# The middle fourteen steps of a fused pose, memory and expert kernel: loop or written out

## What is computed

```
# part 1, per frame: three graph attention layers over the 50 joints, 4 heads
for W, a_s, a_d, bg, R, g, b in layers:            # widths 3 -> 64 -> 128 -> 64
    h = x @ W                                       # per head
    e = leaky_relu(score_src[src] + score_dst[dst], 0.2)
    alpha = softmax of e over the edges that end in a joint
    out = sum over those edges of alpha * h[src]  + bg
    x = gelu(layer_norm(out + x @ R, g, b))
pose = layer_norm(x.reshape(frames, 50*64) @ fpW + fpb)
# part 2, per token (pose tokens and text tokens together, layer-normed)
q = l2norm(silu(causal_conv4(silu(x @ w_q1.T) @ w_q2.T)))
x = x + (silu(q @ mem_w1.T) @ mem_w2.T) @ w_out.T
# part 3, per token: 8 experts 128 -> 512 -> 128 with gelu, the two best of a router weighted
```

## Time and profile before

| | |
|---|---|
| median of 3 runs | 4858.85 us (4856.44 to 4862.07) |
| profiled execution | 4847.68 us |
| its span, first to last instruction | 4845.9 us |
| instructions recorded | 72897 |
| TensorE busy | 88% |
| VectorE busy | 73% |
| ScalarE busy | 54% |
| GpSimd busy | 13% |
| mean granted TensorE clock | 0.964 |

### The profile page before, as it was taken

The page is one execution under the profiler, slowest core; times in us unless marked ns, Lnnn a source line. Parts: engine busy times, 40 slices in busy tenths (PEclk is TensorE's granted clock), DMA queues, the critical chain, the costliest instruction groups (busy, mean ns, idle before and its releaser), DMA issues.

```text
span 4845.9 us, 72897 instructions
## 1 busy us (share of the span) xinstructions
PE 4262.9 (88%) x22774; PEld 1939.4 (40%) x22774; DVE 3549.6 (73%) x8027; ACT 2615.6 (54%) x3930; POOL 627.6 (13%) x746
## 2 busy tenths in 40 slices
PE   4687989898998988989988898988899898899988
PEld 4223343443434334343433434344343433434345
DVE  1577777877778877777887777787777887777762
ACT  0454655556565555655555565555555555565643
POOL 1111201111020111102011120111102011110100
PEclk9898999999999999999999999999999999999998
DMA  2000000000000000000000000000000000000000
GB/s 95 2 1 3 1 3 4 2 5 1 3 4 4 4 2 5 1 3 4 3 4 1 6 1 3 4 3 4 1 4 3 4 4 2 5 1 4 3 2 6
DMA packets 23087, 25.64 MB, mean 5 GB/s; under 512 B 3395, under 2 KB 21835, under 8 KB 22139
## 3 DMA queue, kind: packets, MB, share of 16 engines
q1 hardware_dynamic: 22650, 20.26, 1.3%
HBM read 16.06 MB, written 4.19 MB: 4 GB/s over the span
## 4 chain that ended last, share of the span: by engine, by line
PE 64%; DVE 18%; issue 8%; ACT 7%; POOL 1%; DVEq 0%; SPq 0%; DMA 0%; ACTq 0%; POOLq 0%
PE bank L859 11%; PE bank L812 8%; PE bank L925 7%; PE bank L916 6%; PE bank L696 5%; PE bank L829 4%; PE bank L770 3%; PE bank L850 2%; PE bank L815 2%; ACT X L1264 2%; PE bank L708 2%; DVE X L1870 2%; DVE Ho L2019 2%; PE bank L832 1%; PE bank L846 1%
## 5 line engine op out<-in xcount | busy, mean ns | idle before, releaser
L1870 DVE TENSOR_TENSOR X<-X,bank 128x1024 f32<-128x1024 f32 (+2 forms) x432 | 483.7, 1140 | 268.2 <-PE bank L736 153.2
L1264 ACT ACTIVATE X<-X,c_vec 128x1024 f32<-128x1024 f32 (+2 forms) x432 | 498.3, 1176 | 298.3 <-DVE X L1870 297.2
L1308 ACT ACTIVATE X<-bank,bgc 128x512 f32<-128x512 f32 (+1 forms) x624 | 419.2, 672 | 441.9 <-PE bank L859 441.9
L916 PE MATMUL bank<-XT,c_w 128*128 128x512 f32 x1024 | 509.6, 626 | 28.6 <-ACT SQ L1344 26.6
L925 PEld LDWEIGHTS bank<-c_w,SQ 128*128 128x128 f32 x4096 | 481.9, 192 | 56.5 <-issue 50.2
L925 PE MATMUL bank<-c_w,SQ 128*128 128x128 f32 x4096 | 500.8, 277 | 0.0
L812 PE MATMUL bank<-R,c_W 64*128 64x512 f32 (+1 forms) x832 | 473.3, 650 | 28.4 <-issue 23.3
L532 POOL TENSOR_TENSOR R<-X 128x512 f32<-128x512 f32 (+1 forms) x208 | 257.3, 1241 | 1613.4 <-PE bank L812 838.5
L859 PE MATMUL bank<-R,c_C 128*128 128x512 f32 (+1 forms) x832 | 460.2, 635 | 0.0
L846 PE MATMUL bank<-X,WR 64*128 64x512 f32 (+1 forms) x832 | 455.9, 637 | 0.0
L1344 ACT ACTIVATE SQ<-bank,c_vec 128x512 f32<-128x512 f32 x512 | 345.4, 686 | 164.6 <-PE bank L916 162.5
(11 more groups left out here) (258 smaller groups left out, 6822.5 us busy)
## 6 DMA issues: line engine op xcount, KB each, us to landing
c_w<-in_w SPq DMA_DIRECT2D x2, 2048.0 KB
out<-Ho SPq DMA_DIRECT2D x32, 128.0 KB, 2.6
c_fpW<-in_fpW SPq DMA_DIRECT2D x1, 3200.0 KB
X<-in_x SPq DMA_DIRECT2D x34, 75.0 KB, 1.9
X<-in_txt SPq DMA_DIRECT2D x32, 64.0 KB, 1.8
X<-in_chain SPq DMA_DIRECT2D x1, 1300.0 KB
X<-in_sel SPq DMA_DIRECT2D x1, 600.0 KB
X<-in_sel SPq DMA_DIRECT2D x1, 300.0 KB
```

Of the source, the lines that this page charges most:

```text
L916: mm(hidden_bank(e, m), w1[:, k * P:k * P + P], XT2[:], start=True, stop=True).then_inc(hid_ps, 1)
L1264: A_(dst, dst, ACT.Gelu, bias=v(f"b{l}"), scale=v(f"g{l}")).then_inc(x_ok, 1)
L1308: A_(dst, bZ[k % 2][:, 0:cols], ACT.Identity, bias=bias).then_inc(zs_ok, 1)
L1870: TT(dst, dst, b, ALU.mult).then_inc(u_ok, 1)
```

## The change

Each engine's loop over the steps 1 to 14 becomes a Python loop, so that the fourteen steps are written out one behind the other, with constants in place of the step register. The order of the work, the tiles and the waits stay as they are. On VectorE the counter that `link` waits for becomes a constant as well. The general path keeps its loops.

```
@@ SyncE
-                with sp.Fori(1, STEPS - 1) as s:
+                for s in range(1, STEPS - 1):
                     iteration(s, True, True)
@@ GpSimd
-                with pool.Fori(1, STEPS - 1) as s:
+                for s in range(1, STEPS - 1):
                     iteration(s, True)
@@ TensorE
-                with pe.Fori(1, STEPS - 1) as s:
+                for s in range(1, STEPS - 1):
                     iteration(s, True, True, True)
@@ ScalarE
-                with act.Fori(1, STEPS - 1) as s:
+                for s in range(1, STEPS - 1):
                     iteration(s, True, True)
@@ VectorE
-                with dve.Fori(1, STEPS - 1) as s:
+                for s in range(1, STEPS - 1):
                     start[0] = s * LINKS + (first - LINKS)
                     iteration(s, True, True)
```

## The result

The changed kernel took 4790.13 us (median of 4 runs, 4785.98 to 4797.39), the kernel before 4860.12 us beside it (4 runs): a ratio of 0.9863 [0.9845, 0.988]. Its profiled execution took 4790.66 us, 57.0 us less than that of before.

What follows compares the result with a forecast made beforehand. Engine work plus a pattern of low clock was taken to bound the kernel; 24.7 us for the jumps and 6.8 for the clock made 31.5, giving 4827 us from the median 4858.85, with a range of 4799 to 4853.

Steps and rivals of the forecast that it cites:

- What bounds the kernel: Whole kernel: engines' work fills the span; thirteen looped steps of 287.64 us each are work plus a pattern of low clock.
- The jump, 24.7 us: Loop's back edge on TensorE and VectorE: 13 jumps at 1.9 us each, all on the path, saved by writing out.
- Does the gain hold?: Claim that the lead at the layer's start, 2.09 us, survives to the first variance row (L1844), 2.05 us.
- Registers, nothing: Register instructions computing wait numbers in looped steps: costed at nothing, bound 0.2 us a step, 3 us over fourteen.
- The clock after the pause, 6.8 us: 13.7 us at clock 0.50 behind the restart in 5 of 13 boundaries: 1.4 us each, expected to go with the pause.
- the seam's further lead: Jump-free passage from fourteenth looped step to tail reaches L723 3.14 us earlier, 1.9 explained; the rest counted as nothing.
- The rival of the whole lead: All steps start like the jump-free seam: 47.6 us gain, 4811 us; at the shortest step length 59.4 us, 4799; chance 20%.
- The baseline: Gain summed against the profiled 4847.68 us but subtracted from the timed median 4858.85, 11.2 us above it, giving 4827.
- The slower rival: Clock pattern settles badly, every step falling into the long one: 12.5 us slower, 4871 us; chance 8%.
- The signs: Expected trace: no 3.6 us TensorE branch but the last, L1833 near 7.0 us, mean step near 285.2, busy times unchanged.

Runs made afterwards that it cites:

- e3: Kernel before with only VectorE's fourteen steps written out, the other engines keeping their loops: 4842.1 us, ratio 0.9984.
- e9: Kernel before with TensorE and VectorE written out with constants, loops of ScalarE, GpSimd and SyncE kept: 4806.9 us, ratio 0.9893.
- e5: Changed kernel with the step number taken from a register plus a constant on all engines but SyncE, no loop: 4819.6 us, ratio 0.9918.
- e12: Changed kernel with ten one-column memsets added at the end of each of VectorE's fourteen steps: 4801.2 us, ratio 0.9882.
- e14: Changed kernel with six small matmuls in layer 0's late waits, plus three at each of two waits in layers 1 and 2: 4793.4 us, ratio 0.9854.
- e13: Changed kernel with six small matmuls where TensorE waits late in layer 0's spreading: 4791.4 us, ratio 0.9851.
- e1: Changed kernel with each written-out step in a loop of one trip, its register replaced by constants: 4829.6 us, ratio 0.9935.
- e2: Kernel before with only TensorE's fourteen steps written out, the other four engines keeping their loops: 4911.2 us, ratio 1.0098.
- e6: Kernel before with the loop made seven trips of two steps on every engine, registers kept, six jumps back instead of thirteen: 4866.3 us, ratio 1.0014.
- e7: Kernel before with eight matmuls into a free bank at the end of TensorE's looped step: 4864.6 us, ratio 1.0002.
- e10: Changed kernel with two one-column memsets added at the end of each of VectorE's fourteen steps: 4795.2 us, ratio 0.9875.

## Why the prediction missed

*What bounds the kernel* was right: work plus a pattern of low clock, step by step. Two readings in it were loose. "The same to 1%" holds for VectorE and ScalarE, while TensorE's busy time went from 256.2 to 263.1 us with the clock; and the shortest step was 284.90 us, not 284.97.

*The jump, 24.7 us.* Right: 1.8 to 2.1 us a step at equal clock, 27 us at the most. VectorE's stall is what counts (e3); TensorE's 1.69 us are covered once that is gone, and the other engines' jumps are free on the path (e9).

The Trainium skill (Runtime: NRT & Kernel Launch, section Instruction fetch mechanics) says that a jump to code outside the two buffered blocks must fetch it first. The runs are on the side of this rule: the steps of TensorE, VectorE and ScalarE, with 3073, 932 and 488 instructions recorded in the fourth step, stall at the jump for 2.35 us or more; those of GpSimd and SyncE, with 84 and 23, go on within 0.25 us. The 108 ns that the Trainium skill gives for a compare-and-branch (Advanced Engine Details and Errata, section Control Flow Timing) are not what a jump back of TensorE or VectorE costs here. No run watched the fetch itself.

*Does the gain hold?* Yes, to the step's end.

*Registers, nothing.* Right for the step: 0.06 us in the pair of e5 and e12. My evidence for it was weaker than I took it to be, though. The seam that I compared with has a low stretch of 3.4 us 10.4 us behind the cut (the 0.88 of the earlier trace rows), and such a one costs 0.6 us at L1844 (84.80 against 84.20 us in e14's steps with and without it). From L1833 to L1844, e5 with its registers needs 77.94 and 78.05 us in its two steps without a low stretch at 11 us, and the changed kernel 77.49. So the two equal distances of 2.09 and 2.05 us were in part two differences that cancelled. The bound of 0.2 us a step held for the step's end, not for the place that I read.

*The clock after the pause, 6.8 us.* This is the step that failed: "a low stretch costs 1.4 us net", so "5 x 1.4 = 6.8 us", and with it "I count nothing" for the seam's further lead. Low clock was worth 56.5 - 27.3 = 29 us between the two profiled executions.

The mistake lies in what the low boundary was compared with. The third boundary was at full clock in the 13.7 us behind the restart, and I called it "not low". But it has a low stretch of 3.4 us at 85.9 us behind the cut, ahead of the transposes of L723 where I read the price. So have all eight boundaries of its kind, and the seam has one at 10.4. The 1.4 us were the difference between two patterns, both of them low. From the cut to L723 the second and third steps before have:

```profile
1044.69:1139.53 94.84, 91.27 (x320) 30.80 (x319) 69.92 (x180) 54.54 (x89) 14.25 (x12) 0.93 0.02 4
1332.76:1426.24 93.48, 87.11 (x320) 30.26 (x319) 69.40 (x180) 54.43 (x89) 14.36 (x12) 0.98 0.02 4
```

and the second and first steps of the changed kernel:

```profile
1044.86:1134.34 89.48, 85.41 (x320) 29.30 (x319) 71.30 (x180) 54.27 (x89) 14.21 (x12) 1.00 0.01 4
758.36:849.47 91.11, 87.04 (x320) 29.88 (x319) 71.65 (x180) 54.27 (x89) 14.22 (x12) 0.98 0.01 4
```

Twelve of its thirteen steps come to L723 at 89.48 us with no low stretch on the way, the first at 91.11 with one of 3.4 us at 84. Before, the five low boundaries come there at 94.95 us on average and the other eight at 93.33. With 2.1 us taken off for the jump, a long stretch cost 94.95 - 89.48 - 2.1 = 3.4 us and a short one 93.33 - 89.48 - 2.1 = 1.75; in the changed kernel it cost 1.6. So the head of the step gave 5 x 3.4 + 8 x 1.75 - 1.6 = 29 us, all that was to be explained. Behind L723 nothing was won: the rest of the step takes 193.7 us on average in both kernels.

In the terms of the prediction: 17 us where it had 6.8, for the five; and 14 us, less 1.6, where it had nothing, for the eight. The first part goes with the jump, in these traces at least: stretches that long stand at the head of a step nowhere else. The second is luck, as far as these runs show: the short stretch near 85 us is in all thirteen steps of e13 and in eleven of e1, with no jump at all. The seam's further lead, of which I counted nothing because it "may be luck of the clock", was this too: the third boundary had the stretch at 86 us and the seam had not. Against that boundary a step with no low clock leads by 4.0 us, of which 2.1 are the jump.

What a low microsecond costs depends on where it lies: 3.4/13.7 = 0.25 us in the long stretches at the head, 1.6/3.4 = 0.5 in the short one at 84 us, and (283.53 - 279.67)/10.2 = 0.38 near 251.

The rival of the whole lead, with 47.6 us and 59.4 at the outside, bracketed the 57.0 us of the profiled pair; the 70 us between the medians lie beyond both.

*The baseline.* I summed against one execution and subtracted from the median, noting the 11.2 us between them but not what they meant. That execution was at 0.964 where the runs of before average 0.960: it held less low clock than usual, so part of what the change would win was not in the trace to be read. By medians the clock's share is 70 - 27 = 43 us. Through the clocks of all runs it comes to 0.0128 x 25 = 32 us, or with 0.38 us for each low one (97 us of low time for 0.01 of clock) to 47; the second agrees with it, the first leaves more than the jump can explain.

*The slower rival.* It did not come true for this change, but its mechanism is real: e2 is 1% slower than before with one pause less, of which the later L1833 explains 0.9 of 4.8 us a step, and e6 has half of the jumps gone and no gain.

*The signs.* No jump of 3.6 us, 1.93 us, and the missing low stretch behind the cut came as written. So did the number of instructions. L1833 came at 6.72 instead of 7.0; the mean step at 283.30 instead of 285.2, which the list did not provide for. "Busy times unchanged" failed by 2 us on VectorE (GpSimd holds it up once a step, and the stall hid that) and by the clock on TensorE.

Open: what makes the clock fall where it does. e7, e13 and e14 show that filling waits moves the low stretches; nothing here says which pattern a given version will lock into. Nor was the change tried on a kernel whose steps never see a low clock, where it should give the jump alone.

## What to carry to other kernels

Split a saving in two from the start: the pause itself, from steps whose low stretches lie at the same places, and the clock, from the time at low clock in all steps. Before a step is called "not low", look for low stretches on the whole way to the point where it is read, and not only next to the edit. The pause was forecast here to 3 us. The clock's part can be as large, can have either sign, and a sure-looking change can lose by it. So the range should reach down to steps with no low clock at all: before's own steps give (290.52 - 284.97)/(23.9 - 6.8) = 0.32 us for a low one, and 16.3 x 0.32 x 13 = 68 us, an estimate that could have been made beforehand. Before subtracting from a median, look whether the profiled execution's granted clock is that of the other runs.

## What the runs showed of the hardware

- One jump back stalls VectorE for 2.7 to 3.1 us without a record of its own and is worth 1.8 to 2.1 us a step; TensorE's record reads 3.6 us, and in e3 it cost nothing on the path. ScalarE's stall is 2.35 to 2.65 us; GpSimd and SyncE, with short loops, come back in 0.1 and 0.2 us.
- Execution repeats to 0.02 us from step to step while the clock pattern is the same: e10 has a step of 286.63 to 286.65 us four times.
- Versions whose first product comes 0.33 us later (e1) or 0.11 us later (e10 to e12) took 40 to 48 and 5 to 20 us longer than the changed kernel, nearly all of it at low clock; two measurements of the changed kernel differ by 8.5 us.
- Stretches at 0.50 of 13.7 us and more came at the head of a step only behind TensorE's jump (13 of the 45 such boundaries in before, e3, e6 and e7); not shown is what decides which of them.
- A small VectorE operation that meets GpSimd's L532 takes 1.1 to 1.3 us instead of 0.16. Whether it meets it depends on tenths of a microsecond: in e9 L532 mostly starts up to 0.2 us ahead of the last small operation, which then takes 1.12 to 1.28 us; in one step it starts 0.01 us behind it, the operation takes 0.16 us, and L1833 comes at 5.65 us instead of 6.61.
- The instruction queues moved less for longer code: q14 129 packets against 216, q8 185 against 221.
